# Sums, row spreads and offset convolution on quarters of TensorE's array

## What is computed

```python
def deform(x, w_off, b_off, w, b):            # layer 0; layer 1 multiplies val by sigmoid(mask)
    offset = conv3x3(x, w_off) + b_off         # 18 channels (27 in layer 1)
    py = base_y + ky + off_y; px = base_x + kx + off_x
    val = sum over the 4 corners of x[corner] * (1-|py-y|) * (1-|px-x|), zero outside
    return einsum('bckhw,ock->bohw', val, w) + b
x = x + deform(_gn(x), ...L0)
x = x + relu(gamma * norm1(deform_masked(_gn(x), ...L1)) + beta)
```

## Time and profile before

| | us |
|---|---|
| median of three runs | 170.88 |
| lowest, highest | 170.29, 173.8 |
| the profiled execution | 170.41 |
| its span in the trace | 168.6 |
| TensorE / weight loads busy | 148.6 / 112.4 |
| ScalarE / VectorE / POOL busy | 105.8 / 104.9 / 68.0 |

### The profile page before, as it was taken

The page is one execution under the profiler, slowest core; times in us unless marked ns, Lnnn a source line. Parts: engine busy times, 40 slices in busy tenths (PEclk is TensorE's granted clock), DMA queues, the critical chain, the costliest instruction groups (busy, mean ns, idle before and its releaser), DMA issues.

```text
span 168.6 us, 4694 instructions
## 1 busy us (share of the span) xinstructions
PE 148.6 (88%) x1640; PEld 112.4 (67%) x1640; DVE 104.9 (62%) x248; ACT 105.8 (63%) x243; POOL 68.0 (40%) x131
## 2 busy tenths in 40 slices
PE   7999977999998989997888999998788988979920
PEld 2466634699897766774666876774666867969910
DVE  0526668987675564369986675359975667753133
ACT  3014678889768465379777575379787657864201
POOL 8601355354454434235154434235154425541011
PEclk9999999999999999999999999999999999999996
DMA  5998315200000001520000001520000000020002
GB/s 196 286 251 202 96 34 148 66 2 4 0 6 0 6 2 45 146 60 0 0 4 0 0 8 44 146 61 2 0 6 0 0 10 0 2 70 4 4 6 70
DMA packets 12757, 8.38 MB, mean 50 GB/s; under 512 B 3052, under 2 KB 11820, under 8 KB 12728
## 3 DMA queue, kind: packets, MB, share of 16 engines
q1 hardware_dynamic: 12440, 7.73, 16.9%
q10 hardware_dynamic: 288, 0.27, 0.5%
HBM read 3.31 MB, written 0.59 MB: 23 GB/s over the span
## 4 chain that ended last, share of the span: by engine, by line
PE 72%; DVE 12%; issue 9%; ACT 4%; POOL 1%; POOLq 0%; DVEq 0%; ACTq 0%
PE vb L986 18%; PE ob L1006 18%; PE ob L907 11%; PE ring L943 9%; PE ring L951 8%; DVE s L765 5%; PE vb L1081 3%; ACT xa L575 2%; PE ring L895 2%; DVE msk L718 2%; PE ring L926 2%; DVE pos L711 1%; DVE ytent L757 1%; PE ring L885 1%; ACT off L526 1%
## 5 line engine op out<-in xcount | busy, mean ns | idle before, releaser
L487 POOL TENSOR_SCALAR xa<-xa 125x384 f32<-125x384 f32 x108 | 57.5, 538 | 70.1 <-ACT xa L575 69.5
L765 DVE SCALAR_TENSOR_TENSOR s<-xa,ring 125x384 f32<-125x384 f32 x108 | 58.3, 551 | 32.9 <-PE ring L943 28.8
L575 ACT ACTIVATE xa<-ring 125x384 f32<-125x384 f32 x108 | 51.4, 488 | 17.8 <-PE ring L951 17.0
L1006 PE MATMUL ob<-val,w_d 128*64 128x192 f32 x432 | 42.6, 326 | 0.0
L951 PE MATMUL ring<-pos,soon 68*64 68x384 f16 x216 | 37.5, 329 | 3.8 <-DVE s L765 3.1
L943 PE MATMUL ring<-ytent,soon 128*64 128x384 f16 x216 | 37.4, 328 | 3.1 <-DVE ytent L757 1.3
L986 PE MATMUL vb<-s,shifted 125*64 125x216 f32 (+2 forms) x376 | 34.9, 305 | 0.9 <-DVE s L765 0.9
L1006 PEld LDWEIGHTS ob<-val,w_d 128*64 128x64 f32 x432 | 33.7, 136 | 2.5 <-issue 0.4
L986 PEld LDWEIGHTS vb<-s,shifted 125*64 125x64 f32 x376 | 24.5, 136 | 5.0 <-ACT xa L575 1.3
L598 ACT ACTIVATE val<-vb 128x432 f32<-128x432 f32 x33 | 17.5, 530 | 7.4 <-PE vb L986 6.0
L951 PEld LDWEIGHTS ring<-pos,soon 68*64 68x64 f16 x216 | 14.3, 109 | 9.8 <-issue 3.7
(11 more groups left out here) (77 smaller groups left out, 113.4 us busy)
## 6 DMA issues: line engine op xcount, KB each, us to landing
shifted<-blk SPq DMA_DIRECT2D x8, 200.0 KB
shifted<-blk SPq DMA_DIRECT2D x8, 150.0 KB
shifted<-blk SPq DMA_DIRECT2D x8, 100.0 KB
soon<-c_soon SPq DMA_DIRECT2D x1, 640.0 KB, 7.3
x_l<-x SPq DMA_DIRECT2D x2, 288.0 KB, 4.4
w_o<-w_off SPq DMA_DIRECT2D x2, 288.0 KB, 4.4
w_d<-w_def SPq DMA_DIRECT2D x4, 144.0 KB, 4.2
late<-c_late SPq DMA_DIRECT2D x1, 576.0 KB, 7.2
```

The lines of the kernel that those rows point to most:

```text
L487: nc.gpsimd.tensor_scalar(v, v, 1.0, 0.0, ALU.min, ALU.max).then_inc(xu_ready, 1)
L575: nc.scalar.activation(xa[:, n % XA_BUFS, :], bank("x", n)[0:SPAN, 0:2 * UPX], ACT.Abs).then_inc(act_took, 1)
L765: nc.vector.scalar_tensor_tensor(out=s[u % 2][:, k // 3:k // 3 + 2 * THIRD, W * k:W * (k + 1)], in0=xa[:, n % XA_BUFS, :].rearrange("q (r ...
L1006: last = mm(sums[64 * i:64 * i + 64, 0:UPX], w_d[l][:, t, 64 * i:64 * i + 64], val[u % 2][:, t // 3:t // 3 + THIRD, W * t:W * (t + 1)], st ...
```

## The change

- `weighted` runs on quarters of the array: for each tap four matmuls of 64 lanes, 64 columns and 96 pixels. Bank `ob[:, 0]` gets the upper half of the unit's rows with each image in its own lanes, `ob[:, 1]` the lower half with the images' lanes exchanged. Three instructions take the sums out instead of one (`SUMS`). `w_d` holds no zeros now.
- `row_spread` reads 64 lanes: the tents of even taps lie in lanes 0 to 63, of odd taps in 64 to 127. `column_spread`, `y` and `mask` read 60 and 59 lanes instead of 68 and 91.
- `conv` runs as one job: for each tap eight matmuls of 64 lanes, 32 columns and 144 pixels (image i, quarter q), each image into its own bank of `ring`. `off` is taken out in two instructions and has two buffers.
- The convolutions of both first stages stand whole in the head; norm(1) stands before them.
- `windows` is issued in half chunks, and the slots of nearly all jobs are new. The final mean and variance use `ring`.

```diff
-OFF_LANES = 68
+OFF_LANES = 60
-MLO = 64
+MLO = 32
-YLO = 64
-YROWS = 2 * YLO
+YLO = 32
+YROWS = 128
+def tent_lane(k, part):
+    return 64 * (k % 2) + YLO * part + ROWS * (k // 2)
 UNIT = {
-    "x": {"PE": -26, "ACT": -26, "POOL": -22}, "s": {"PE": -22, "DVE": -22}, "windows": {"PE": (-1, 2, 4, 6)},
-    "values": {"ACT": (0, 2, 4, 6)}, "weighted": {"PE": (10, 10, 11, 11, 12, 13, 13, 13, 14)},
-    "sums": {"ACT": 14, "DVE": 19}, "summed": {"DVE": 20},
+    "x": {"PE": -26, "ACT": -26, "POOL": -21}, "s": {"PE": -22, "DVE": -22},
+    "windows": {"PE": (-1, 0, 0, 1, 5, 6, 6, 6)}, "values": {"ACT": (0, 2, 6, 6)},
+    "weighted": {"PE": (8, 10, 10, 11, 11, 12, 13, 13, 13)}, "sums": {"ACT": 13, "DVE": 17}, "summed": {"DVE": 18},
 }
 LAST_UNIT = {
-    "windows": {"PE": (-11, -10, -8, -3, -2)}, "values": {"ACT": (-10, -9, -7, -2, -1)},
-    "weighted": {"PE": (-2, -2, -2, -1, -1, -1, 2, 2, 2)},
+    "windows": {"PE": (-12, -11, -10, -10, -9, -4, -3, -3, -2, -2)}, "values": {"ACT": (-12, -11, -9, 0, 1)},
+    "weighted": {"PE": (0, 0, 0, 1, 1, 2, 4, 4, 4)},
 }
 LAYER = {
-    "xt": {"PE": (6, 7), "ACT": (6, 7)}, "conv": {"PE": (7, 8, 9, 9, 11, 13, 18, 18, 19)}, "offsets": {"ACT": 18},
+    "xt": {"PE": (6, 7), "ACT": (6, 7)}, "conv": {"PE": 13, "ACT": 13}, "parts": {"DVE": 12},
...
-HEAD_PE = [("idle", 11), ("norm", 0), ("idle", 3), ("idle quarters", 3), ("idle", 2), ("xt", (0, 0)), ("xt", (0, 1))] + [("conv", (0, k)) for k in range(5)] \
-    + [("norm", 1)] + [("conv", (0, k)) for k in range(5, TAPS)] + [("conv", (1, k)) for k in range(5)] + [("y", (0, 0))]
-HEAD_ACT = [("xt", (0, 0)), ("xt", (0, 1)), ("offsets", 0)] \
-    + [("split", (0, q)) for q in range(4)] + [("y", (0, 0))]
+HEAD_PE = [("idle", 12), ("norm", 0), ("idle", 4), ("xt", (0, 0)), ("xt", (0, 1)),
+           ("norm", 1), ("conv", 0), ("conv", 1), ("y", (0, 0))]
+HEAD_ACT = [("xt", (0, 0)), ("xt", (0, 1)), ("conv", 0), ("split", (0, 0)), ("split", (0, 1)), ("split", (0, 2)),
+            ("y", (0, 0)), ("split", (0, 3)), ("conv", 1)]
...
-        w_o = [sb(f"w_o{l}", [128, TAPS, 64]) for l in range(LAYERS)]
-        w_d = [sb(f"w_d{l}", [128, TAPS, 128]) for l in range(LAYERS)]
+        w_o = [sb(f"w_o{l}", [128, TAPS, 32]) for l in range(LAYERS)]
+        w_d = [sb(f"w_d{l}", [128, TAPS, C]) for l in range(LAYERS)]
...
+        SUMS = [(0, slice(0, 128), slice(0, 128), 0), (1, slice(64, 128), slice(0, 64), 1), (1, slice(0, 64), slice(64, 128), 1)]
...
-            sp.wait_ge(cleared, 7)
...
-            for l in range(LAYERS):
-                nc.gpsimd.memset(w_d[l][:, :, :], 0.0).then_inc(cleared, 1)
...
-                nc.scalar.activation(off[:, :], conv_bank(m)[:, 0:HALF], ACT.Identity, bias=b_off[l]).then_inc(t_free, 1)
+                for i in range(2):
+                    wait_full(act, "conv", (m, i))
+                    nc.scalar.activation(off[m % 2][:, QPX * i:QPX * (i + 1)], bank("conv", (m, i))[:, 0:QPX], ACT.Identity, bias=b_off[l])\
+                        .then_inc(act_took, 1)
...
-                nc.scalar.activation(y[:, p, UPX * j:UPX * (j + 1)], sums[:, 0:UPX], ACT.Identity, bias=b_def[l])\
-                    .then_inc(sums_taken, 1)
+                for b, there, own, h in SUMS:
+                    nc.scalar.activation(y[own, p, half_rows(j, h)], ob[there, b, 0:UPX // 2], ACT.Identity, bias=b_def[l][there, :])\
+                        .then_inc(sums_taken, 1)
...
-                for h in range(2):
-                    last = mm(conv_bank(m)[64 * h:64 * h + 64, 0:HALF], w_o[l][:, t, :],
-                              pixels(rows_from(m, 12 * h + t // 3, t % 3, 12), 12),
-                              start=t == 0, stop=t == TAPS - 1)
+                for t in range(TAPS):
+                    for i in range(2):
+                        for q in range(QUARTERS):
+                            own = slice(C * i, C * i + C)
+                            last = mm(bank("conv", (m, i))[32 * q:32 * q + 32, 0:QPX], w_o[l][own, t, :],
+                                      pixels(rows_from(m, own, QROWS * q + t // 3, t % 3, QROWS), QROWS),
+                                      start=t == 0, stop=t == TAPS - 1)
...
             def row_spread(n):
                 u, k = divmod(n, TAPS)
+                half = slice(64 * (k % 2), 64 * (k % 2) + 64)
                 for d in range(2):
-                    last = mm(bank("s", n)[64 * d:64 * d + 64, 0:2 * UPX], sel[:, k, 64 * d:64 * d + 64],
-                              ytent[u % 2][:, :, :], start=True, stop=True)
+                    last = mm(bank("s", n)[64 * d:64 * d + 64, 0:2 * UPX], sel[half, k, 64 * d:64 * d + 64],
+                              ytent[u % 2][half, :, :], start=True, stop=True)
...
-                for i in range(2):
-                    last = mm(sums[64 * i:64 * i + 64, 0:UPX], w_d[l][:, t, 64 * i:64 * i + 64],
-                              val[u % 2][:, t // 3:t // 3 + THIRD, W * t:W * (t + 1)],
-                              start=t == 0, stop=t == TAPS - 1)
+                for h in range(2):
+                    for i in range(2):
+                        own, to = slice(C * i, C * i + C), C * (i ^ h)
+                        last = mm(ob[to:to + C, h, 0:UPX // 2], w_d[l][own, t, :],
+                                  val[u % 2][own, t // 3 + THIRD // 2 * h:t // 3 + THIRD // 2 * (h + 1), W * t:W * (t + 1)],
+                                  start=t == 0, stop=t == TAPS - 1)
```

239 lines of the change are left out of this document (113 added, 126 removed).

## The result

| | before | after | forecast |
|---|---|---|---|
| median of the runs side by side, us | 172.34 | 175.12 | 155.0 |
| lowest, highest | 170.29, 173.9 | 174.08, 176.47 | 149 to 163 |
| ratio, 95% interval | | 1.026 [1.015, 1.038] | 0.91 |
| profiled execution, its span | 170.41, 168.6 | 174.08, 172.2 | 153.0 (span) |
| mean granted clock of TensorE | 0.99 | 0.925 | |

A forecast was written before the change was run, and what follows sets the result against it. TensorE's streaming, busy 148.6 of 168.6 us, was taken as the bound. Stage gains less drains, evictions and waits came to -15.6 us off 170.4, giving 154.8, stated as 155; own range 151 to 160, 8 in 10 from 149 to 163.

The forecast's parts named there:

- Part 1: Sums on quarters: a tap goes from 0.325 to 0.17 us, 1.40 us less a unit, 16.7 us of TensorE.
- Rival (b): Sums: row halves writing one bank take turns, a tap stays at 0.32; 167 us, chance of 164 to 169 0.09.
- Part 2: Spreads: odd row spreads run beside their neighbour, hiding 0.16 us each, 0.65 us a unit, 7.7 us in all.
- Part 3: Convolution in 16 records a tap, taken at 0.29 us a tap; 1.7 us less for each of four, 7 us.
- Part 4: Drains at changes of matmul shape on TensorE: 0.13 us each, 0.8 us a unit, 9.4 us in all, a cost.
- Part 5: More evictions: three for a unit's sums, +0.6 us on ScalarE or VectorE; `off` in two of 0.37, +0.25.
- step 1: TensorE in plain units: time taken off its streaming counts nearly in full; unit 8.25 us, 0.95 less.
- -1.9, -3.9, -3.7 and -1.8: Forecast changes in us: two plain units, two stretches of three units with a convolution, two units from 133 to 150.
- rival (a): Plain units: ScalarE, VectorE and TensorE wait in turn over four banks, stopping at 8.8 us; 161.6 us, chance 0.16.
- step 2: Plain units: windows 4 to 7 in one run, sums following while ScalarE still has two copies, cost +0.3 us.
- step 3: Head and first unit: -2.8 us, 2 up to the first windows and 0.8 more until 37.9.
- the drains: Rival on changes of shape: 72 more at 0.5 us each lose 5 us; 175 us, chance of above 171 0.04.

The follow-up runs named there:

- experiment 1: The run of half_spreads: row spreads on 64 lanes and column spreads on 60, on the kernel before; 184.53 us, ratio 1.083.
- Experiment 5: late_shifts with part of ScalarE's distances, of VectorE's sum evictions, or of both left out; 170.3, 174.12, 168.3 us; plain units 9.2, 9.0, 8.8 us.
- old_slots: Changed kernel with a unit's windows and values back in four separate slots instead of one run of windows; 177.62 us, ratio 1.037 against the kernel before.
- half_spreads: Kernel before with only the spreads changed: row spreads on 64 lanes by parity, column spreads on 60; 184.53 us, ratio 1.083.
- hold_clock: Changed kernel with 15 idle matmuls put before the spreads where TensorE waits between 17 and 22 us; 178.71 us, ratio 1.044 against the kernel before.
- conv_only: Changed kernel with sums, spreads and unit order as before; quartered convolution, new head and stages' slots left; 180.15 us, ratio 1.052 against the kernel before.
- sums_conv: conv_only plus the sums on quarters, in three runs between spreads of 128 lanes; 179.67 us, no ratio given.
- late_shifts: Changed kernel with SP's shifted image copies held back until the stage's convolution is done; 171.41 us, ratio 0.998 against the kernel before.

## Why the prediction was wrong

**Right: every price of an instruction.** The sums of the last unit, x72, and the three evictions of a sum, after:

```profile
161.82 1.72 PE L1022 MATMUL ob<-val,w_d 64*64 64x96 f32 x72 [0.18 <-issue]
...
53.80 1.01 DVE L787 SCALAR_TENSOR_TENSOR x_mid<-ob,vec,x_l 128x96 f32<-128x96 f32 x3
```

- Part 1: (1.72 - 0.25)/71 is 20.7 ns a record, 0.17 us a tap, as read from the earlier trace rows. Rival (b) falls with it: two row halves write one bank, into different lanes, at full speed. The Trainium skill (TensorEngine Tiling (Array Packing), Gotcha 1: PSUM Pressure) has it that different row tiles can't access the same bank at once; in the form measured here, with different lanes of the bank, they did without loss, and the measurement decides.
- Part 2: 0.01 against 0.16 for odd row spreads, right (experiment 1).
- Part 3: 15.4 ns a record, 0.25 us a tap, under my 0.29; the stream's own floor was the right end to take.
- Part 4: 0.12 to 0.15 us a change, right.
- Part 5: 1.01 us for the three instead of 0.41, right; `off` 0.38 each, right.

**Wrong, step 1: "what is taken from TensorE's streaming counts nearly in full".** This is the premise on which -1.9, -3.9, -3.7 and -1.8 rest, and it is rival (a) that came true, stronger than I had sized it: plain units of 9.4, not 8.8. TensorE did shed its time (16.32 us busy in two units instead of 18.26, idle 2.4 instead of 0.4), but the unit got no shorter: VectorE and ScalarE have 7.4 and 7.5 us of work in it, and with spreads, distances, clamps, samples and tents passing four banks in a fixed order, a wait of one can become a wait of all. The row that I leaned on, a chain that never left TensorE, says who is last today. It doesn't say how far behind the next one is: ScalarE and VectorE idled 2.2 and 3.1 us a unit, and I took this idle time for slack. Experiment 5 splits the 1.15 us by which the unit exceeds the forecast: about half is the load of these two, the other half remains without it. What holds that half is argued, not shown.

**Wrong, step 2: the new order costs 0.3.** Windows 4 to 7 in one run starve VectorE for 1.38 us; I had looked at ScalarE's copies behind that run and not at who gets no spreads during it. Yet putting the slots back gave only 0.26 and 0.05 us in the two plain units (old_slots), so this is the smaller part.

**Wrong, step 3: the head, -2.8 forecast, +4.9 measured.** The marks on the way, in us (the forecast's where it names them):

| | before | forecast | after | half_spreads |
|---|---|---|---|---|
| conv(0) starts | 8.94 | 9.6 | 10.44 | 9.37 |
| `y` | 16.62 | 15.1 | 17.02 | 17.17 |
| first distance | 17.40 | 16.8 | 18.93 | 17.95 |
| first windows | 28.06 | 26 | 30.39 | 30.13 |
| unit 0's result | 40.5 | 37.7 | 45.4 | 45.4 |

Four things, none in my sum:
- The idle filler, put at nothing. The channel statistics are there at 5.6, but norm(0) starts at 6.18, behind the twelve idle matmuls (before at 5.59). With norm(1) conv(0) then starts 0.8 us later than forecast.
- The stop of 1.69 us inside conv(1). I counted the time of 288 matmuls at 15 to 21 ns and not that an engine has to be given 288 instructions at that rate.
- TensorE with little to do until 20.6. The forecast counted the emptier TensorE there as harmless ("TensorE no longer has four taps of conv(1) between the first spreads"). In the earlier trace rows, TensorE had conv until 16.8; it was busy 17.55 of the first 18.9 us before and 13.27 after (the rows above).
- The clock. TensorE's level fell from 2.4 to 1.2 GHz at 20 us, after gaps of 1.69 and 1.38 us and within one of 1.03 (19.5 to 20.6), and stayed there until 37, also while TensorE was busy 4.00 of 4.00 us. hold_clock sets the price of this at 2.1 us or more of unit 0's time.

It would be wrong to lay all of it on the new head. half_spreads has the old one, with the four taps of conv(1) between the spreads and without a stop, and it too lost its clock (0.50 from 23.8 to 34.0) and had unit 0's result at 45.4. And conv_only and sums_conv, with the new head and spreads of the old form, lost the clock too (0.50 from 23.1 to 36.7 and from 21.9 to 32.1). So part 2 alone brings the fall, and so do part 3 and the head without part 2; the forecast had put both at nothing for the clock. Of the 7.7 us, 2.1 were lost up to the first distance, with the filler and the stop; how the 5.6 behind it divide between low clock, changes of shape and waits isn't known.

**Wrong, step 4: nothing for the clock elsewhere.** No rival had it. Every variant of the changed kernel has a mean clock of 0.885 to 0.937 in its profile, half_spreads 0.958, against 0.99 before. In sums_conv the low clock falls into the unit with the convolution, which takes 4.1 us longer than before, some 2.4 of them stops. After itself had such a fall at 78 us, for 3.4 us, behind the stop that ended at 75.8.

**The chances.** Faster 0.90 came from cases that all agreed on one thing, that TensorE's shed time is a gain of some size; they differed in how much. The case that ended slower was the drains, the one price in doubt that was measured right. A case "TensorE gets emptier, and the kernel is slower for it" was missing. The part of it without the clock was to be had from the earlier trace rows: 18.9 to 37.9, with no engine above 16.4 of 19.0 us, was already a stretch in which less work on TensorE could bring nothing. (The chances above 163, as they stand, add up to about 0.17 and not 0.14.)

**What stays open.** How the 4.9 us of the head divide between stop, clock, changes of shape and waits; part 1 alone on the kernel before, with its head, convolution and spreads, was not run, so whether the quarters of the sums gain without the rest is untested. Why the clock falls again at 64 us in one variant (hold_clock) and at 139 in another (late_shifts) isn't settled, nor is what brought it down in half_spreads. Whether an order exists that keeps the 8.8 us units of sums_conv and fills the stretches with a convolution; the best that was tried, late_shifts, is equal to the kernel before, 0.998 [0.993, 1.004], and no version that does all the work beat it.

## What to carry to other kernels

A chain that stays on one engine tells who is last, and what the runner-up needs tells how much can be won: before counting a microsecond off the busiest engine, rebuild the unit with that engine's work taken out and see who waits for whom through the shared buffers. Cutting large matmuls into many small ones can be right to the nanosecond per record and still lose, by instructions that don't arrive in time, by 0.12 to 0.15 us for each change of shape, and by a lower granted clock. Here the clock fell both where gaps of 1 to 1.7 us had opened and, in half_spreads, where the gaps were as before; so after any such change look at the granted clock first, and in a forecast price one stretch at half speed. And try each part alone on the old kernel before ascribing a loss to the part that looks guilty.
